# A graph network kernel: 125 instead of 100 of every 500 nodes are summed from gathered rows, and the rest from counts

## The chip, the core and the metric

The kernel runs on one core of a Trainium2 chip. The metric is the device time of one execution in microseconds; below it is the median of three runs. Stretches and single instructions are read from one execution that was profiled.

## What is computed

There are 12,500 nodes with 64 features, and 212,500 directed edges (src, dst, 16 attributes), sorted by dst. Each of three layers is a convolution; after the first two comes a ReLU, and the result of the third is added to x and normalized per row:

```
m = concatenate([h[dst], h[src], edge_attr], axis=1) @ W + b
conv(h) = segment_sum(m, dst, 12500)
h = relu(conv(x, W1, b1)); h = relu(conv(h, W2, b2)); out = layernorm(x + conv(h, W3, b3))
```

Since W acts on sums as well as on single rows, the kernel needs three things per node: the sum of the source rows over its incoming edges, the sum of their attributes, and its degree times its own row.

## The kernel before, in words

The nodes are cut into 100 tiles of 125 (`TILES`, `L`) and 25 batches of four tiles, 500 nodes (`BATCHES`, `B`). A step g is a batch in a layer, 75 steps in all. The sum over sources is made in two ways.

For the first 400 nodes of a batch (`DENSE`) it is a product with a matrix of counts: `blocks[:, k, t, s]` says how many edges go from each of the 125 nodes of tile t to node s. The source rows are held as three bf16 parts (`parts`), and per tile TensorE does one wide matmul with the first two parts (`apply_wide`, L1093) and one narrow one with the third (`apply_narrow`, L1101), narrow ones alternating between the two halves of the array. All add up in one PSUM bank. The counts are built once, during layer 0, for the next batch while the present one is applied: VectorE makes a key mask for a chunk of 5 nodes (`make_key`, L909; every fifth time `make_low`, L899), TensorE multiplies the two masks (`build_chunk`, L1074), ScalarE writes 101 pieces of 5 fp8 values (`keep_counts`, L779). That is 80 builds a batch. When a batch is complete, ScalarE's queue stores it to DRAM (`store_counts`, L787), and in layers 1 and 2 SP's queue loads it back in four quarters (`load_block`, L554), two batches ahead.

For the last 100 nodes (`FAR` = 2 groups of `GW` = 50) the source rows are gathered: GpSimd issues `J` = 8 indirect DMAs per group, one edge per partition each (`gather_rows`, L673), and TensorE multiplies them with a mask of the targets (`sum_far`, L1125 wide and L1129 narrow). In layers 1 and 2 `gather_batch` puts three pauses of two plain operations each among the 16 gathers (`rest`, L682).

The attributes are summed in layer 0 in ten groups of 50 nodes. SP loads a group three ahead (`load_group`, L578 and L584, a ring of four), GpSimd splits it into three bf16 parts (`split_attr`, L700, L702, L705, L707), VectorE makes the mask (`make_mask`, L926), TensorE sums eight times (`sum_attr`, L1114).

Order is written out by hand. In layer 0 TensorE goes through ten units of ten tiles with eight builds among them; a unit ends with the narrow matmuls and one attribute group, the last one with `sum_far` too. The first four builds of the next batch are done ahead of its first apply. VectorE goes through 80 keys and does other work at given keys: `keep_acc` of the batch before at key 1 (L948, it waits for `far_summed`, and TensorE's next apply waits for it), `keep_attr` at 6, `keep_h` at 11, `look` at 18, `make_nodes` at 53 (L974), masks at 5, 13, 21 and so on. GpSimd splits group k, issues two gathers, and ends with `make_rows` of the batch before (L717, rows times degrees for the next layer) and `scale_rows` (L728). In layers 1 and 2 each step of GpSimd is `gather_batch(g + 1)` and then, up to the first step of layer 2, `make_rows(g - 1)`; the gathers wait until the far sums two batches before are done. ScalarE copies the accumulator and the own rows (L804, L806), and then waits for `make_rows` with the store of the rows; the next batch's copy is queued behind it. TensorE's `conv` (L1154, L1155) of a batch comes in the second and third quarter of the next one and waits for those copies.

A group that has more edges than its 1,024 slots is found by `flags`, and a slow branch then does the whole work.

## Time and profile before

| | us |
|---|---|
| median of 3 runs | 3171.07 (3166.14 to 3173.89) |
| the profiled execution | 3200.72 |
| its span, first to last instruction | 3198.8 |
| TensorE busy (matmul) | 2854.0, 89% |
| GpSimd busy | 2312.6, 72% |
| VectorE busy | 1467.0, 46% |
| ScalarE busy | 1245.1, 39% |

Busy time of an engine leaves out register, semaphore and DMA-issuing work. A mean duration of a matmul is longer than its distance to the next, since matmuls are pipelined. Layer 0 with the builds ends at about 1586 us, its last batch at 1634; layer 1 ends at 2426 and layer 2 at 3188.

### The profile page before, as it was taken

Reading aid. Unit: us, or ns where it says so; the run is one execution under the profiler, and the core shown is the slowest. Engines: PE = TensorE matmul, PEld = TensorE weight load, DVE = VectorE, ACT = ScalarE, POOL = GpSimd, SP = SyncE. Lnnn points to the kernel's source line nnn. Section 1 sums busy time; section 2 is a strip of 40 time slices with the busy share of each in tenths; the row PEclk is TensorE's granted clock in tenths of the full one; section 3 lists DMA queues with packets and bytes.
Section 4 is the critical chain, followed back from the end, with each engine's and each line's share of the span. In section 5 each row is a group of like instructions: output and inputs, shape, how many; then the busy total and the mean of one; then the engine's idle time right before and its main releaser. Section 6 shows DMA issues by size and latency. Waiting matters only on the chain.

```text
span 3198.8 us, 62003 instructions
## 1 busy us (share of the span) xinstructions
PE 2854.0 (89%) x22952; PEld 1707.3 (53%) x22952; DVE 1467.0 (46%) x3427; ACT 1245.1 (39%) x2139; POOL 2312.6 (72%) x2868
## 2 busy tenths in 40 slices
PE   0049999999999999999985999999999899999998
PEld 0025555555555555555553566666665556666665
DVE  5478888888888888888710110110110111111111
ACT  1058888888888888888600000000000000000000
POOL 2726888888888888878847887777774876766672
PEclk9999999999999999999997999999999999999999
DMA  2134344443535344353586899999997889999992
GB/s 53 33 76 146 105 150 114 127 138 102 162 100 161 103 141 124 108 153 100 161 209 143 203 216 213 215 217 214 216 219 194 186 204 213 210 210 215 214 212 65
DMA packets 276171, 507.31 MB, mean 159 GB/s; under 512 B 179175, under 2 KB 227650, under 8 KB 247750
## 3 DMA queue, kind: packets, MB, share of 16 engines
q1 hardware_dynamic: 174271, 289.44, 35.7%
q10 hardware_dynamic: 58404, 150.91, 16.9%
q0 software_dynamic: 43200, 62.97, 11.0%
q8 instruction: 190, 3.11, 0.5%
q14 instruction: 106, 0.87, 0.1%
HBM read 351.58 MB, written 151.51 MB: 157 GB/s over the span
## 4 chain that ended last, share of the span: by engine, by line
PE 65%; POOL 15%; DVE 6%; DMA 6%; issue 5%; ACT 2%; another core or an unknown queue 1%; SPq 0%; ACTq 0%; POOLq 0%; DVEq 0%
PE ps L1093 32%; PE ps L1101 17%; PE ps L1074 8%; POOL far_rows L673 6%; DMA dst_stage<-in_dst 5%; PE ps L1154 2%; POOL blocks L659 2%; PE ps L1155 2%; DVE is_key L909 2%; ACT blocks L779 1%; POOL attr_stage L702 1%; DVE blocks L847 1%; POOL attr_parts L707 1%; PE ps L1125 1%
## 5 line engine op out<-in xcount | busy, mean ns | idle before, releaser
L1093 PE MATMUL ps<-blocks,parts 125*128 125x400 fp8e4 x7500 | 1674.8, 337 | 7.1 <-DVE acc_sb L948 2.7
L673 POOL DMA_INDIRECT far_rows<-parts,far_src x1200 | 1257.5, 1048 | 460.3 <-issue 322.5
L779 ACT ACTIVATE blocks<-ps 125x505 fp8e4<-125x505 f32 x2000 | 1161.8, 733 | 216.5 <-PE ps L1074 182.3
L1093 PEld LDWEIGHTS ps<-blocks,parts 125*128 125x128 bf16 x7500 | 748.2, 101 | 463.3 <-issue 35.4
L1074 PE MATMUL ps<-is_key,is_low 128*125 128x505 bf16 x2000 | 772.3, 392 | 78.5 <-DVE is_key L909 61.6
L1101 PE MATMUL ps<-blocks,parts 125*64 125x400 fp8e4 x7500 | 722.6, 336 | 0.1
L909 DVE TENSOR_SCALAR is_key<-from_one,parts 128x500 bf16<-128x500 f16 x2000 | 685.7, 391 | 30.6 <-PE ps L1074 26.0
L974 DVE COPY z<-ps 125x256 f32<-125x256 f32 x75 | 31.8, 424 | 1350.4 <-remote 792.9
L1101 PEld LDWEIGHTS ps<-blocks,parts 125*64 125x64 bf16 x7500 | 387.4, 110 | 320.8 <-issue 162.1
L1074 PEld LDWEIGHTS ps<-is_key,is_low 128*125 128x125 bf16 x2000 | 276.6, 139 | 333.7 <-DVE is_key L909 142.6
L804 ACT COPY acc_sb<-ps 128x500 f32<-128x500 f32 x50 | 28.8, 576 | 835.2 <-PE ps L1129 512.3
L899 DVE TENSOR_TENSOR is_low<-from_one,parts 128x625 bf16<-128x625 f16 x400 | 327.9, 820 | 36.8 <-PE ps L1074 24.3
L682 POOL TENSOR_SCALAR attr_stage<-attr_stage 128x256 f32<-128x256 f32 x300 | 260.6, 869 | 15.4
L700 POOL CAST attr_parts<-attr_stage 128x128 bf16<-128x128 f32 x250 | 96.2, 385 | 166.9 <-PE ps L1114 107.8
L707 POOL TENSOR_TENSOR attr_parts<-attr_stage,attr_parts 128x128 bf16<-128x128 f32 x250 | 175.4, 702 | 20.0
L812 ACT ACTIVATE std<-var,eps 125x4 f32<-125x4 f32 x25 | 7.4, 297 | 428.1 <-DVE var L991 412.8
L717 POOL TENSOR_SCALAR node_rows<-z,node_deg 125x64 f32<-125x64 f32 x200 | 127.8, 666 | 58.7 <-DVE z L974 51.5
L1061 PE MATMUL ps<-ident,blocks 125*128 125x125 f32 x40 | 7.2, 366 | 178.1 <-DVE blocks L890 178.1
L702 POOL TENSOR_TENSOR attr_stage<-attr_stage,attr_parts 128x128 f32<-128x128 f32 x250 | 145.3, 581 | 20.5
L806 ACT COPY own_sb<-ps 64x500 f32<-64x500 f32 x50 | 28.4, 569 | 283.0 <-PE ps L1140 264.5
L1154 PE MATMUL ps<-w_src,acc_sb 128*125 128x64 f32 x600 | 125.0, 290 | 6.7 <-ACT own_sb L806 6.7
L926 DVE SCALAR_TENSOR_TENSOR masks<-dst_stage,from_one 128x400 bf16<-128x400 int32 x200 | 114.9, 575 | 28.4 <-DMA dst_stage<-in_dst 26.7
(101 smaller groups left out, 1432.4 us busy)
## 6 DMA issues: line engine op xcount, KB each, us to landing
blocks<-counts SPq DMA_DIRECT2D x100, 1137.5 KB
counts<-blocks ACTq DMA_DIRECT2D x25, 4375.0 KB
blocks<-counts SPq DMA_DIRECT2D x100, 1050.0 KB
far_rows<-parts,far_src POOLq DMA_INDIRECT x1200
attr_stage<-in_edge_attr SPq DMA_DIRECT2D x250, 64.0 KB
blocks<-counts SPq DMA_DIRECT2D x100, 132.0 KB
counts<-blocks ACTq DMA_DIRECT2D x25, 507.8 KB
blocks<-counts SPq DMA_DIRECT2D x100, 121.9 KB
```

The lines of the kernel that those rows point to most:

```text
L673: nc.gpsimd.indirect_dma_start(far_rows[:, g % 2, h, j, :], None, parts_d[layer], bass.IndirectOffsetOnAxis(ap=far_src[:, g % BATCHES, h, ...
L682: nc.gpsimd.tensor_scalar(attr_stage[:, 2:4, :], attr_stage[:, 0:2, :], 1.0, None, ALU.mult).then_inc(rested, 1)
L702: nc.gpsimd.tensor_tensor(values, values, attr_parts[:, turn, :, 0:ED], ALU.subtract).then_inc(attr_left, 1)
L707: nc.gpsimd.tensor_tensor(attr_parts[:, turn, :, 2 * ED:3 * ED], values, attr_parts[:, turn, :, ED:2 * ED], ALU.subtract).then_inc(attr_sp ...
L717: last = nc.gpsimd.tensor_scalar(node_rows[:, g % 2, t, :], z[:, t, :], 0.0, deg[:, n:n + 1], ALU.max, ALU.mult)
L779: nc.scalar.activation(blocks[0:L, b % 2, :, n * W:(n + 1) * W], build[0:L, c % BUILD, 0:COLS].rearrange("p (t w) -> p t w", w=W), ACT.Cop ...
L899: nc.vector.tensor_tensor(is_low[:, m % 2, :, :], from_one[:, 0:L].rearrange("p (a l) -> p a l", a=1).to_broadcast([P, LOWS, L]), lows[:, ...
L909: nc.vector.tensor_scalar(is_key[:, c % KEY_RING, 0:KEYS], from_one[:, :], keys[:, b, n:n + 1], None, ALU.is_equal).then_inc(keyed, 1)
L1074: nc.tensor.matmul(build[0:L, c % BUILD, 0:COLS], is_low[:, c // LOWS % 2, c % LOWS, :], is_key[:, c % KEY_RING, 0:COLS], start=True, stop ...
L1093: nc.tensor.matmul(acc_ps(g), parts[0:L, layer % 2, t, 0:2, :].rearrange("p k d -> p (k d)"), blocks[0:L, g % 2, t, :], start=(t == 0), st ...
L1101: last = nc.tensor.matmul(acc_ps(g)[side:side + D, :], parts[0:L, layer % 2, t, 2, :], blocks[0:L, g % 2, t, :], start=False, stop=(t >= T ...
L1154: nc.tensor.matmul(z_ps[:, t, :], acc_flat[:, at], w_src[layer][:, :], start=True, stop=False)
```

## The change

A far group is now one whole tile: 125 nodes of each batch are gathered, in `FJ` = 18 gathers, and 375 are counted (`FAR`, `DENSE`). The builds are 75 a batch. The attributes are summed in six groups a batch: five near ones of 75 nodes (`NEAR`, `J` = 11) and the far one of 125 (18). The far mask is one operation, in fp8. The rows of `blocks` are 375 bytes long without padding. The pauses come at gathers 0, 6 and 12. `keep_acc` moves from key 1 to key 4. SP stores the attributes and loads rows and the far sources earlier in the batch. `make_rows` and `scale_rows` stay on GpSimd, `make_rows` behind the fifth group, `scale_rows` behind the sixth.

```diff
-    GW = 50
-    FAR = 2
-    DENSE = B - FAR * GW
+    FAR = 125
+    DENSE = B - FAR
+    NEAR = 5
+    GW = DENSE // NEAR
     BUILDS = DENSE // W
-    BLOCK = (TILES + 1) * DENSE
+    COLUMNS = (TILES + 1) * DENSE
+    BLOCK = -(-COLUMNS // 4) * 4
-    PAUSES = [0, 5, 10]
+    PAUSES = [0, 6, 12]
-    J = 8
+    J = 11
+    FJ = 18
-    PER_BATCH = B // GW
+    PER_BATCH = NEAR + 1
+    UNITS = TILES // UNIT
+    SUM_AFTER = [1, 3, 4, 6, 8, 9]
+    MASK_AT = [BUILDS * u // UNITS + 5 for u in SUM_AFTER]
+    GATHERS = [FJ * k // NEAR for k in range(NEAR + 1)]
...
-        far_rows = sb("far_rows", [P, 2, FAR, J, PARTS * D], bf16)
-        far_masks = sb("far_masks", [P, 2, FAR, J, GW], bf16)
+        far_rows = sb("far_rows", [P, 2, FJ, PARTS * D], bf16)
+        far_masks = sb("far_masks", [P, 2, FJ, FAR], fp8)
...
                     if g >= 1:
-                        if k == 1:
+                        if k == 0:
                             store_attr(sp, g - 1)
-                        elif k == 2 and g + 1 < BATCHES:
+                        elif k == 1 and g + 1 < BATCHES:
                             load_h(sp, g + 1)
-                        elif k == 3 and g + 1 < BATCHES:
                             load_far(g + 1)
...
             def gather_batch(g):
-                for i in range(FAR * J):
-                    if i in PAUSES:
+                for j in range(FJ):
+                    if j in PAUSES:
                         rest()
-                    gather_rows(g, i // J, i % J)
+                    gather_rows(g, j)
...
-                    if k < PER_BATCH - FAR:
-                        for i in range(k * FAR * J // (PER_BATCH - FAR), (k + 1) * FAR * J // (PER_BATCH - FAR)):
-                            gather_rows(g, i // J, i % J)
-                    if k == 7 and g:
+                    if k < NEAR:
+                        for j in range(GATHERS[k], GATHERS[k + 1]):
+                            gather_rows(g, j)
+                    if k == 4 and g:
                         make_rows(g - 1)
-                    if k == 8:
+                    if k == 5:
                         scale_rows(g)
...
                 nc.vector.scalar_tensor_tensor(
+                    out=far_masks[:, g % 2, :, :],
+                    in0=far_dst[:, b, :].rearrange("p (j a) -> p j a", a=1).to_broadcast([P, FJ, FAR]),
+                    scalar=float(b * B + DENSE - 1),
+                    in1=from_one[:, 0:FAR].rearrange("p (a n) -> p a n", a=1).to_broadcast([P, FJ, FAR]),
+                    op0=ALU.subtract, op1=ALU.is_equal, saturate=False).then_inc(masked, 1)
...
-                    if g >= 0 and n % BUILT == 5:
-                        make_mask(g, n // BUILT)
+                    if g >= 0 and n in MASK_AT[0:NEAR]:
+                        make_mask(g, MASK_AT.index(n))
+                    if g >= 0 and n == MASK_AT[NEAR]:
+                        make_far_masks(g)
                     if g >= 1:
-                        if n == 1:
+                        if n == 4:
                             keep_acc(g - 1)
...
+                for j in range(FJ):
+                    nc.tensor.matmul(acc_ps(g, at), far_rows[:, g % 2, j, 0:2 * D], far_masks[:, g % 2, j, :],
                                      start=(j == 0), stop=False)
+                for j in range(FJ):
                     side = j % 2 * D
...
-                        sum_attr(g, u)
-                        if u == PER_BATCH - 1:
-                            for h in range(FAR):
-                                sum_far(g, h)
+                        if u in SUM_AFTER:
+                            sum_attr(g, SUM_AFTER.index(u))
+                        if u == UNITS - 1:
+                            sum_far(g)
```

## Rows read from the trace of the kernel before

**Rows 1.** The page, part 5, ScalarE's evictions: busy us, mean ns | idle before, releaser

```profile
L779 ACT ACTIVATE blocks<-ps 125x505 fp8e4<-125x505 f32 x2000 | 1161.8, 733 | 216.5 <-PE ps L1074 182.3
```

**Rows 2.** Windows by stage: length, each engine's busy us, granted clock, DMA share, GB/s

```profile
303.50:1586.40 1282.90, 1213.01 (x9476) 726.15 (x9474) 1085.29 (x2643) 1070.33 (x1840) 1056.83 (x1474) 0.98 0.45 129
...
1862.40:2425.70 563.30, 563.30 (x4789) 341.70 (x4789) 57.15 (x133) 21.76 (x39) 413.91 (x471) 1.00 0.91 214
...
2654.90:3188.20 533.30, 533.30 (x4536) 323.52 (x4534) 73.91 (x178) 25.96 (x55) 346.81 (x372) 1.00 0.86 195
```

**Rows 3.** Groups of TensorE by shape: busy us, mean ns | idle before, releaser

```profile
L1093 PE MATMUL ps<-blocks,parts 125*128 125x400 fp8e4 x7500 | 1674.8, 337 | 7.1 <-DVE acc_sb L948 2.7 <-issue 2.2 <-ACT blocks L779 1.9
...
L1114 PE MATMUL ps<-masks,attr_parts 128*49 128x50 bf16 x1600 | 75.4, 186 | 4.4 <-POOL attr_parts L707 4.4
L1125 PE MATMUL ps<-far_masks,far_rows 128*128 128x50 bf16 x1200 | 57.4, 187 | 44.0 <-DMA far_rows<-parts,far_src 43.9
...
L1140 PE MATMUL ps<-ident,h_rows 125*64 125x125 f32 x300 | 46.3, 277 | 0.8 <-issue 0.8
```

**Rows 4.** Timeline of TensorE in layer 1: start, length, what, count

```profile
1943.32 4.56 PE L1093 MATMUL ps<-blocks,parts 125*128 125x400 fp8e4 x26
1947.82 2.39 PE L1101 MATMUL ps<-blocks,parts 125*64 125x400 fp8e4 x26
1950.14 0.38 PE L1125 MATMUL ps<-far_masks,far_rows 128*128 128x50 bf16 x8
...
1951.24 4.24 PE L1093 MATMUL ps<-blocks,parts 125*128 125x400 fp8e4 x24
```

**Rows 5.** Timeline of TensorE at a batch boundary of layer 0

```profile
911.50 0.64 PE L1074 MATMUL ps<-is_key,is_low 128*125 128x505 bf16 x2
914.67 1.11 PE L1074 MATMUL ps<-is_key,is_low 128*125 128x505 bf16 x2 [2.54 <-DVE is_key L909]
915.57 1.87 PE L1093 MATMUL ps<-blocks,parts 125*128 125x400 fp8e4 x5
```

**Rows 6.** Timeline of VectorE before and at that boundary

```profile
900.56 0.56 DVE L926 SCALAR_TENSOR_TENSOR far_masks<-far_dst,from_one 128x400 bf16<-128x400 int32 x1
...
907.05 0.83 DVE L899 TENSOR_TENSOR is_low<-from_one,parts 128x625 bf16<-128x625 f16 x1
907.80 0.86 DVE L909 TENSOR_SCALAR is_key<-from_one,parts 128x500 bf16<-128x500 f16 x2
913.68 0.68 DVE L948 COPY acc_sb<-ps 128x500 f32<-128x500 f32 x1 [5.03 <-remote]
```

**Rows 7.** Timeline of ScalarE's queue at that boundary

```profile
910.90 0.77 ACTq L787 DMA_DIRECT2D counts<-blocks  x2
```

**Rows 8.** Timeline of GpSimd, layer 1: first gather, and one steady batch

```profile
1671.89 1.04 POOL L673 DMA_INDIRECT far_rows<-parts,far_src  x1 [24.26 <-issue]
...
2010.81 1.03 POOL L673 DMA_INDIRECT far_rows<-parts,far_src  x1 [1.49 <-PE ps L1129]
2012.14 0.94 POOL L673 DMA_INDIRECT far_rows<-parts,far_src  x1 [0.30 <-issue]
...
2034.63 2.43 POOL L717 TENSOR_SCALAR node_rows<-z,node_deg 125x64 f32<-125x64 f32 x4 [0.35 <-issue]
...
2040.46 1.02 POOL L673 DMA_INDIRECT far_rows<-parts,far_src  x1 [1.50 <-PE ps L1129]
```

**Rows 9.** Groups of GpSimd in the window 310 to 1580 us

```profile
L673 POOL DMA_INDIRECT far_rows<-parts,far_src x364 | 451.7, 1241 | 90.9 <-issue 77.2 <-PE ps L1114 1.5
L707 POOL TENSOR_TENSOR attr_parts<-attr_stage,attr_parts 128x128 bf16<-128x128 f32 x227 | 163.5, 720 | 18.2
...
L700 POOL CAST attr_parts<-attr_stage 128x128 bf16<-128x128 f32 x228 | 89.0, 391 | 80.9 <-PE ps L1114 56.5 <-DMA dst_stage<-in_dst 24.1
```

**Rows 10.** Timeline of GpSimd in layer 0, two-input operations of a split

```profile
865.42 0.42 POOL L702 TENSOR_TENSOR attr_stage<-attr_stage,attr_parts 128x128 f32<-128x128 f32 x1
...
866.28 2.94 POOL L707 TENSOR_TENSOR attr_parts<-attr_stage,attr_parts 128x128 bf16<-128x128 f32 x1
```

More of the change, by code:

```diff
@@ L57, in gnn_kernel @@
     BANK = 512
-    assert TABLE_Q <= BANK and COLS <= BANK and E % P and GROUPS % PER_BATCH == 0
+    assert TABLE_Q <= BANK and COLS <= BANK and E % P and NEAR * GROUP_CHUNKS * W == DENSE
     PARTS = 3
@@ L1110, in sum_attr @@
                     pe.wait_ge(attr_kept, b)
-                h = k - (PER_BATCH - FAR)
-                mask = masks[:, group % 2, :, :] if h < 0 else far_masks[:, b % 2, h, :, :]
-                for j in range(J):
-                    last = nc.tensor.matmul(attr_ps[:, k * GW:(k + 1) * GW],
-                                            attr_parts[:, group % 2, j, 0:AROWS], mask[:, j, :],
-                                            start=(j == 0), stop=(j == J - 1))
-                last.then_inc(attr_summed, 1)
@@ L1119, in sum_far @@
-            def sum_far(g, h):
-                at = slice(DENSE + h * GW, DENSE + (h + 1) * GW)
-                pe.wait_ge(masked, far_group(g, h) + 1)
-                pe.wait_ge(far_landed[g % 2], (g // 2 + 1) * FAR * J * DMA)
-                for j in range(J):
-                    nc.tensor.matmul(acc_ps(g, at), far_rows[:, g % 2, h, j, 0:2 * D], far_masks[:, g % 2, h, j, :],
+                js = J if k < NEAR else FJ
+                at = slice(k * GW, (k + 1) * GW) if k < NEAR else slice(DENSE, B)
@@ new lines, in sum_attr, with sum_far @@
+                mask = masks[:, group % 2, :, :] if k < NEAR else far_masks[:, b % 2, :, :]
+                for j in range(js):
+                    last = nc.tensor.matmul(attr_ps[:, at], attr_parts[:, group % 2, j, 0:AROWS], mask[:, j, :],
+                                            start=(j == 0), stop=(j == js - 1))
+                last.then_inc(attr_summed, 1)
+            def sum_far(g):
+                at = slice(DENSE, B)
+                pe.wait_ge(masked, far_group(g) + 1)
+                pe.wait_ge(far_landed[g % 2], (g // 2 + 1) * FJ * DMA)
+                for j in range(FJ):
+                    nc.tensor.matmul(acc_ps(g, at), far_rows[:, g % 2, j, 0:2 * D], far_masks[:, g % 2, j, :],
@@ L1126, in sum_far @@
                                      start=(j == 0), stop=False)
-                for j in range(J):
+                for j in range(FJ):
                     side = j % 2 * D
-                    last = nc.tensor.matmul(acc_ps(g, at)[side:side + D, :], far_rows[:, g % 2, h, j, 2 * D:3 * D],
-                                            far_masks[:, g % 2, h, j, :], start=False, stop=(j >= J - 2))
+                    last = nc.tensor.matmul(acc_ps(g, at)[side:side + D, :], far_rows[:, g % 2, j, 2 * D:3 * D],
+                                            far_masks[:, g % 2, j, :], start=False, stop=(j >= FJ - 2))
@@ L1160, in _ @@
             for g in range(-1, BATCHES):
-                for u in range(PER_BATCH):
+                for u in range(UNITS):
                     unit = range(u * UNIT, (u + 1) * UNIT)
@@ L1166, in _ @@
                         if g + 1 < BATCHES:
-                            for n in range(u * BUILT + i * BUILT // UNIT, u * BUILT + (i + 1) * BUILT // UNIT):
+                            t = u * UNIT + i
+                            for n in range(t * BUILDS // TILES, (t + 1) * BUILDS // TILES):
                                 if not (ahead and n < 4):
@@ L1208, in _ @@
                         elif q == 1:
-                            for h in range(FAR):
-                                sum_far(g - 1, h)
+                            sum_far(g - 1)
                         elif q == 2:
@@ L1221, in _ @@
                 if g % BATCHES:
-                    for h in range(FAR):
-                        sum_far(g, h)
+                    sum_far(g)
                 if g == BATCHES:
```

126 lines of the change are left out of this document (59 added, 67 removed).

## The prediction

> **What bounds the kernel now.** I read the page first, then the kernel in windows by stage [rows 2], because a share of the whole span hides that three engines take turns. In layer 0 (303.5 to 1586.4 us, 23 batches by the copies of L948) a batch takes 1282.9/23 = 55.8 us; TensorE is busy 95% of it, VectorE 85%, ScalarE 83%, GpSimd 82%, so none is far from being the bound. In the steady part of layer 1 (563.3 us, 19 batches) and of layer 2 (533.3 us, 18 batches) a batch takes 29.65 us, TensorE is never idle at granted clock 1.00, and GpSimd looks free (73% and 65%). That last number misleads: each gather is followed by 0.30 us in which the engine counts as idle ("issue") [rows 8]. The reader is to see in [rows 8] that in layer 1 GpSimd starts a batch of gathers at 2010.81 and the next at 2040.46, and that only 1.50 us of these 29.65 are a wait for TensorE. GpSimd's own work is 28.15 us a batch: it is 5% from being the bound of layer 1. Transfers take 0.91 and 0.86 of the DMA engines' time there [rows 2], without a wait that TensorE shows.
>
> At the batch boundary of layer 0 TensorE starts two chunk builds at 911.50, then idles 2.54 us until 914.67, and applies the next batch's first tile at 915.57 [rows 5]. VectorE had made two keys and was waiting in `keep_acc` until 913.68, although the last far matmul was started before 911.50 [rows 6]. ScalarE issued the store of the counts at 910.90 [rows 7]; I can't tell whether that is what holds the signal back. After such a gap 5 wide matmuls take 1.87 us, 0.33 us each against 0.17, so the clock is at its lower level, 1.2 GHz. In the layer-0 window the mean clock is 0.98, that is 4% of 1283 us at half speed, 26 us lost, 1.1 us a batch.
>
> **TensorE, per batch.** The pitch of a matmul is (length of a run minus the mean of one)/(count minus 1). Wide, 400 columns: (4.56-0.337)/25 = 0.169 us; that is 400 columns at 0.417 ns (2.4 GHz, granted clock 1.00) and 3 ns beside them [rows 3, 4]. I price every long matmul so; a chunk build of 505 columns is 0.214 us. Narrow matmuls run in pairs on two halves of the array, 13 pairs in the 2.32 us up to the next run: a pair in 0.17 us and some 0.1 us for the change of shape [rows 4].
> - Apply: 25 columns fewer in 100 wide and 50 narrow pairs: 150 x 0.0104 = -1.56 us.
> - Far sums before: 1951.24 - 1950.14 = 1.10 us for two runs each of 8 wide and 8 narrow [rows 4]. After: 18 wide of 125 columns, 0.055 us each, with the change of shape 1.08 us; 9 narrow pairs of 0.059 us and the change 0.63 us. +0.61 us. The 0.055 is what the columns take; the ceiling is the nearest row with 125 columns, L1140, fp32: 75 runs of four in 46.3 us are 0.62 each, (0.62-0.277)/3 = 0.114 us. I take the floor, since at 50 columns the weight load of the same shape hides in 0.027 us [rows 3]; the ceiling adds 18 x 0.059 + 9 x 0.055 = 1.6 us.
> - Net in layers 1 and 2: -0.95 us, 29.65 to 28.7.
> - Layer 0 only: five builds fewer, -5 x 0.214 = -1.07. Attributes: 80 matmuls of 50 columns at 0.027 (0.38 us for eight, L1114 has a mean of 0.186) = 2.16 us become 55 of 75 columns at 0.034 and 18 of 125 at 0.055 = 2.86, +0.70; the changes of shape stay as many as the units. Net -0.95 - 1.07 + 0.70 = -1.3 us; clean work of TensorE falls from some 50.9 to 49.6 us, the other 4.9 of the 55.8 being stalls and half clock.
> - The rows of `blocks` now start every 375 bytes instead of 400, at odd addresses. No row shows such a read. Price between nothing and unknown; ScalarE already writes 5-byte pieces at odd offsets and takes 1161.8/2000 = 0.58 us [rows 1]. I take nothing and make it a rival.
>
> The Trainium skill, "TensorE: Matmul & The Clock Gate", section "Back-to-back issue gap", says that pairs of weight load and matmul sustain about 81 ns at 128 columns, not the 55 that columns alone give. It speaks against this change, which trades cheap columns in long matmuls for short ones; the 0.027 us at 50 columns [rows 3] doesn't show such a floor.
>
> **The boundary of layer 0.** `keep_acc` moves from key 1 to key 4, so the four builds that TensorE does ahead (0.86 us) no longer wait behind the copy. Before, two builds at the low clock (0.90 us) stood between the copy and the first apply; they go. The last attribute group and the far sums are 0.7 + 0.6 = 1.3 us longer, but they fill time in which TensorE idles now if the signal is held until about the same moment after the store's issue. From 4.6 us above clean work in this batch (2.54 idle, 0.5 more than normal in two late builds, and some 1.6 of half clock, of which five wide matmuls alone are 0.8) I keep 1 to 2. Over all boundaries I count -2.1 us a batch, half clock included; bounds -0.5 (only the key wait goes) and -4.
>
> **VectorE.** Near masks: 5 of 825 elements instead of 8 of 400; far mask: one of 2250 instead of two of 400. A 400-element mask takes 0.56 us [rows 6]. If 0.15 us of it are fixed (between nothing and all, an element costs at most 1.4 ns) 1.0 and 2.5 us: 7.5 against 5.6 us. Five keys of 0.34 and a set of lows of 0.8 us [rows 6] go, -2.5 us. Sum -0.6 us, about 46 of the new batch. The far mask stands before key 73; queued behind it are the last keys, for which TensorE waits; the ring of six keys covers some 3.4 us, the mask takes 2.5. I allow 0.2 us. It has then 5 us for waits, of which `keep_acc` takes some 4: it is as tight as before, and this, not the columns, keeps me from forecasting more.
>
> **GpSimd in layer 0.** Two more gathers: 1.24 busy [rows 9] and 0.25 idle (90.9/364) each, +3.0 us. Splits: 10 groups of 128 elements to 5 of 176 and one of 288. The four operations of a group take about 2.1 us (L700 0.391 and L707 0.720 are two of them) and 0.2 between them, 23 us a batch. If time goes with elements they become 20.4, if it is fixed 13.8; I take 18 (about a third fixed). Net -2: from 55.8 - 56.5/23 - 24.1/23 = 52.3 us of own time [rows 9] to about 50.5. This is under what I forecast for TensorE, by 1 us only. The Trainium skill, "GPSIMD Engine Reference", section "Elementwise — side-by-side cycle accounting", has 2.6 cycles an element for two inputs; as an estimate of that page 0.28 of the 0.42 us that a two-input operation of 128 elements takes without contention [rows 10] are elements, and the sum comes out at the same 18. ScalarE loses 5 x 0.58 = 2.9 us and stays below all.
>
> The attribute loads are issued three groups ahead; a group now lasts 8.7 instead of 5.5 us, so the cover grows. SP's queue issues four groups fewer a batch (eight DMAs), and one source list instead of two.
>
> Layer 0: 49.6 clean + about 2.8 of stalls = 52.4, -3.4 us a batch, x24 = -82 us. First batch of builds, paced by ScalarE: -3. Batch 24, paced by GpSimd: -3. Storing and reloading smaller counts ahead of layer 1: -2. The three are rough: five evictions of 0.58 [rows 1], two batches in which fewer splits meet more gathers, 6% fewer bytes. Together -90 (bounds -40 and -140).
>
> **Layer 1.** GpSimd's 28.15 us gain two gathers of 0.94 + 0.30: 30.65; with `make_rows` at some 2.2 instead of 2.43 us, as I take for a GpSimd that never waits, 30.4. TensorE wants 28.7. So GpSimd becomes the bound: its `make_rows` of one batch is queued behind the gathers two batches on, ScalarE's store waits for it and its copy of the accumulator is queued behind that store, and TensorE's `conv` waits for the copy. The layer begins with GpSimd behind, its first gather at 1671.89 after an idle 24.26 us [rows 8], so no lead has to be used up. 25 gather batches of 28.1 and 22 `make_rows` of 2.2 set the end, where today GpSimd waits. Today the layer ends 2425.7 - 1671.9 = 753.8 us after it; I get 700 + 49 + 3 for the copy + 16 for the half batch behind it = 768: +14 us (bounds +5, +28).
>
> **Layer 2** has no `make_rows`: GpSimd 28.1, TensorE 28.7. The two batches at its start wait for gathers, +5; 23 batches give -0.95 each, -22. -17 us (bounds 0 and -24). DMA: blocks -6%, gathers +12%, a little less in sum than the 0.91 of today.
>
> **Sum.** -90 + 14 - 17 = -93 us against the profiled execution of 3200.7 (span 3198.8). It lies 30 us above the median 3171.07; I put the same difference on the median: 3078 us.
>
> **Rivals.**
> - GpSimd binds layer 0 too. For: its margin is 1 us, and contention lengthens its operations (2.94 us instead of 0.42 in [rows 10]). Against: they may be mostly fixed. Period 54, -43 - 8 + 14 - 17: 3117 us. 0.20.
> - Short matmuls cost more than their columns. By the ceiling's half, 0.8 us in 48 batches of layers 0 and 2 and 0.5 in the attributes, +50: 3128 us. By 81 ns (the Trainium skill, as above) it would be 0.7 and 0.5, much the same. Against: 0.027 us at 50. 0.09.
> - The boundary stall and the half clock go wholly, and VectorE keeps up: period 50.2, -134: 3030 us. 0.11.
> - Slower: odd row addresses slow the streaming of `blocks`. 11,250 wide matmuls and pairs; layer 1 hides 1.5 us a batch, so above about 12 ns each beyond today's rate per column the gain is gone; at 20 ns, +225 - 38 hidden - 93 = +94: 3265 us. Against: nothing in the rows; for: nothing either. 0.07.
> - Nothing moves, because gather time given to layers 1 and 2 eats layer 0: 0.03. That the fallback branch is taken is excluded: counted from the inputs, the largest near group has 1370 edges (1408 fit), the largest far one 2222 (2304 fit).
>
> My forecast has 0.50. A difference of 0.3% (10 us) is about what the measurement can tell. Faster 0.89, same 0.04, slower 0.07. The range 3025 to 3140 leaves out the slower case and the ends of the others.
>
> **What would show it.** Right: layer 1's steady batch at 30 to 30.8 us with TensorE idle at `conv`, released by ScalarE's copy; layer 2's at 28.7; layer 0's at 52 to 52.8; L1093's mean down 10 ns; far matmuls 55 ns apart. Wrong: wide matmuls above 0.16 us apart; layer 0's `sum_attr` waiting for GpSimd's splits; a gap at the boundary still above 2 us.

## The result, and the profile after

The changed kernel takes 3157.84 us (median of 15, 3150.93 to 3166.92), the kernel before, run beside it 15 times, 3171.07. The ratio is 0.996, 95% interval 0.9946 to 0.9973: 13 us faster, where 93 were forecast. The profiled execution of after took 3159.32, its span is 3157.5.

Windows by stage of after, cut at copies of the accumulator as [rows 2] are. The columns are the stretch, its length, the busy time of TensorE's matmuls, of its weight loads, of VectorE, ScalarE and GpSimd, then granted clock, DMA share and GB/s:

```profile
301.60:1509.40 1207.80, 1161.51 (x9292) 721.01 (x9292) 1116.70 (x2409) 1023.73 (x1725) 1066.34 (x1148) 1.00 0.46 130
1800.80:2340.30 539.50, 508.25 (x4352) 325.36 (x4352) 73.32 (x102) 17.69 (x35) 442.15 (x477) 0.97 0.81 194
2616.70:3117.90 501.20, 494.87 (x4353) 319.93 (x4352) 95.91 (x153) 24.52 (x52) 404.53 (x408) 1.00 0.86 199
```

The first is 23 batches of layer 0: 52.5 us each, from 55.8 [rows 2], with the clock up from 0.98 to 1.00. The second is 17 batches of layer 1: 31.7 us each, from 29.65, and TensorE, never idle before, now is for 31 us, with a mean clock of 0.97. The third is 17 of layer 2: 29.5, from 29.65. So layer 0 came out as forecast (52.4), layer 1 not at all (30.4), and layer 2 little better than before (28.7).

TensorE at the end of a batch of layer 2, to be read against [rows 4], and GpSimd's and VectorE's groups of layer 0 (310 to 1500 us) against [rows 9] and [rows 6]:

```profile
2763.20 4.05 PE L1098 MATMUL ps<-blocks,parts 125*128 125x375 fp8e4 x24
...
2788.31 2.27 PE L1106 MATMUL ps<-blocks,parts 125*64 125x375 fp8e4 x26
2790.52 1.20 PE L1130 MATMUL ps<-far_masks,far_rows 128*128 128x125 fp8e4 x18
2791.65 0.69 PE L1134 MATMUL ps<-far_masks,far_rows 128*64 128x125 fp8e4 x18
2792.27 0.98 PE L1098 MATMUL ps<-blocks,parts 125*128 125x375 fp8e4 x5
```

```profile
L677 POOL DMA_INDIRECT far_rows<-parts,far_src x408 | 510.9, 1252 | 107.4 <-issue 96.9 <-PE ps L1120 2.1
L708 POOL TENSOR_TENSOR attr_stage<-attr_stage,attr_parts 128x176 f32<-128x176 f32 x113 | 121.9, 1078 | 9.2
...
L925 DVE SCALAR_TENSOR_TENSOR masks<-dst_stage,from_one 128x825 bf16<-128x825 int32 x114 | 114.8, 1007 | 0.0
L940 DVE SCALAR_TENSOR_TENSOR far_masks<-far_dst,from_one 128x2250 fp8e4<-128x2250 int32 x22 | 54.8, 2493 | 0.0
```

From 2763.20 to 2792.27 is TensorE's own batch, 29.07 us. Masks cost 1.01 and 2.49 us where 1.0 and 2.5 were forecast, a gather in layer 0 1.25 where 1.24 was. L708 is one of four operations of a split; the eight rows of splits add up to 380.5 us, 16.8 a batch, forecast 18.

Layer 1's long waits in after (engine, what it waited for, us, times, longest), 1800.8 to 2340.3 us:

```profile
ACT acc_sb L808 <- POOL node_rows L721: 490.0, 16, 31.0
...
PE ps L1159 <- ACT own_sb L810: 30.0, 16, 2.5
```

That is the chain of the prediction: TensorE's `conv` waits for ScalarE, whose copy stands behind the store that waits for GpSimd's `make_rows`. GpSimd itself never waits for TensorE here. Its timeline over one batch of layer 1, to be read against [rows 8]:

```profile
1904.58 1.81 POOL L686 TENSOR_SCALAR attr_stage<-attr_stage 128x256 f32<-128x256 f32 x2
1906.66 1.09 POOL L677 DMA_INDIRECT far_rows<-parts,far_src  x1 [0.27 <-POOL attr_stage L686]
1908.05 2.51 POOL L677 DMA_INDIRECT far_rows<-parts,far_src  x1 [0.31 <-issue]
1910.86 0.94 POOL L677 DMA_INDIRECT far_rows<-parts,far_src  x1 [0.30 <-issue]
...
1924.94 1.94 POOL L721 TENSOR_SCALAR node_rows<-z,node_deg 125x64 f32<-125x64 f32 x4
```

and VectorE's in the same microseconds:

```profile
1906.90 0.43 DVE L985 TENSOR_TENSOR parts<-left,parts 125x256 bf16<-125x256 f32 x1
1907.24 2.50 DVE L940 SCALAR_TENSOR_TENSOR far_masks<-far_dst,from_one 128x2250 fp8e4<-128x2250 int32 x1
```

Seventeen gathers of this batch take 0.94 to 1.09 us, one takes 2.51. It starts 0.8 us into VectorE's 2.50 us far mask and ends at 1910.56, 0.82 us after the mask. There is one such gather in every batch of that window (17, of 2.1 to 3.2 us). In layers 1 and 2 together 46 gathers start while the far mask runs, and 45 of them end 0.81 to 0.82 us after it, whatever their start. In the steady batches of layer 1 of before (1862.4 to 2396 us), whose masks take 0.56, none takes over 1.1 us.

### The profile page after: what moved, and what is told of

The parts are those of the page before. It is cut to its first block, busy times and chain, and to the rows that moved or that the text cites. A ratio compares the mean times of both kernels' runs of the same rounds, so it can differ in the third digit from the quotient of the medians.

```text
span 3157.5 us, 59682 instructions
## 1 busy us (share of the span) xinstructions
PE 2788.2 (88%) x22952; PEld 1754.3 (56%) x22952; DVE 1570.1 (50%) x3129; ACT 1192.8 (38%) x2014; POOL 2481.3 (79%) x2618
## 4 chain that ended last, share of the span: by engine, by line
POOL 63%; issue 14%; PE 12%; DVE 8%; ACT 2%; DMA 1%; POOLq 0%; ACTq 0%; SPq 0%; DVEq 0%
POOL far_rows L677 39%; POOL attr_stage L686 8%; POOL node_rows L721 4%; PE ps L1098 4%; POOL attr_stage L708 4%; DVE is_key L917 3%; PE ps L1079 3%; PE ps L1106 2%; POOL attr_parts L710 2%; POOL blocks L663 2%; POOL attr_parts L712 2%; ACT blocks L783 1%; DVE blocks L851 1%; DVE is_low L907 1%; POOL attr_parts L706 1%
## 5 line engine op out<-in xcount | busy, mean ns | idle before, releaser
L677 POOL DMA_INDIRECT far_rows<-parts,far_src x1350 | 1489.1, 1103 | 408.7 <-issue 356.3
L1098 PE MATMUL ps<-blocks,parts 125*128 125x375 fp8e4 x7500 | 1563.6, 327 | 3.8 <-ACT blocks L783 2.1
L783 ACT ACTIVATE blocks<-ps 125x505 fp8e4<-125x505 f32 x1875 | 1111.8, 774 | 187.4 <-PE ps L1079 186.9
L1079 PE MATMUL ps<-is_key,is_low 128*125 128x505 bf16 x1875 | 716.0, 391 | 33.2 <-DVE is_key L917 31.3
L1106 PE MATMUL ps<-blocks,parts 125*64 125x375 fp8e4 x7500 | 685.8, 326 | 0.0
L1079 PEld LDWEIGHTS ps<-is_key,is_low 128*125 128x125 bf16 x1875 | 257.5, 138 | 240.0 <-DVE is_key L917 77.4
L940 DVE SCALAR_TENSOR_TENSOR far_masks<-far_dst,from_one 128x2250 fp8e4<-128x2250 int32 x75 | 187.4, 2499 | 0.0
L721 POOL TENSOR_SCALAR node_rows<-z,node_deg 125x64 f32<-125x64 f32 x200 | 156.4, 812 | 38.8 <-DVE z L977 36.7
L1159 PE MATMUL ps<-w_src,acc_sb 128*125 128x64 f32 x600 | 126.0, 292 | 52.2 <-ACT own_sb L810 52.2
L708 POOL TENSOR_TENSOR attr_stage<-attr_stage,attr_parts 128x176 f32<-128x176 f32 x150 | 154.4, 1030 | 12.4
L1159 PEld LDWEIGHTS ps<-w_src,acc_sb 128*125 128x125 f32 x600 | 90.3, 190 | 100.3 <-ACT own_sb L810 60.2
L1130 PE MATMUL ps<-far_masks,far_rows 128*128 128x125 fp8e4 x1350 | 94.0, 225 | 56.3 <-DMA far_rows<-parts,far_src 55.9
L925 DVE SCALAR_TENSOR_TENSOR masks<-dst_stage,from_one 128x825 bf16<-128x825 int32 x125 | 125.9, 1008 | 9.1 <-DMA dst_stage<-in_dst 9.1
```

Of the source, the lines that this page charges most:

```text
L677: nc.gpsimd.indirect_dma_start(far_rows[:, g % 2, j, :], None, parts_d[layer], bass.IndirectOffsetOnAxis(ap=far_src[:, g % BATCHES, j:j + ...
L708: nc.gpsimd.tensor_tensor(values, values, into[0], ALU.subtract).then_inc(attr_left, 1)
L721: last = nc.gpsimd.tensor_scalar(node_rows[:, g % 2, t, :], z[:, t, :], 0.0, deg[:, n:n + 1], ALU.max, ALU.mult)
L783: nc.scalar.activation(blocks[0:L, b % 2, :, n * W:(n + 1) * W], build[0:L, c % BUILD, 0:COLS].rearrange("p (t w) -> p t w", w=W), ACT.Cop ...
L940: nc.vector.scalar_tensor_tensor(out=far_masks[:, g % 2, :, :], in0=far_dst[:, b, :].rearrange("p (j a) -> p j a", a=1).to_broadcast([P, F ...
L1079: nc.tensor.matmul(build[0:L, c % BUILD, 0:COLS], is_low[:, c // LOWS % 2, c % LOWS, :], is_key[:, c % KEY_RING, 0:COLS], start=True, stop ...
```

## The experiments

Each was run beside the kernel before; times are medians. Over five sets of runs the kernel before took 3168.8 (e1 to e4), 3169.6 (e5 to e8), 3200.6 (e9 to e12), 3167.6 (e13 to e16) and 3199.3 us (e17, e18). Two of the sets are thus 30 us slower from the start, and compare only within themselves; what differs in their traces is told with e12.

**e1: no far mask on VectorE from the third batch of layer 1.**

```
if g >= BATCHES + 2:
    nc.vector.engine_nop().then_inc(masked, 1)
    return
```

> The changed kernel, but from the third batch of layer 1 on VectorE no longer builds the far mask (an empty instruction signals in its place, and the mask of two batches earlier is used, so the far sums of these batches are not the reference's). Theory A: the 2.50 us VectorE instruction holds back the GpSimd gather that is issued beside it (2.51 us instead of 0.94). Then all 18 gathers of a batch take 0.94, GpSimd's batch in layer 1 falls from 31.6 to about 30.1 us and in layer 2 from 29.3 to 28.1, where TensorE's own 29.1 binds: 23 x 1.5 + 24 x 0.2 = 39 us less, about 3119. Rival B: the long gather is a matter of its place in the queue (a full ring, the eighth of its batch) and not of VectorE: it stays at 2.5 us and the time at 3158. Rival C: TensorE's columns set layers 1 and 2: the time stays even where the gather shortens.

3114.27 us, ratio to before 0.9829 (0.9812 to 0.9845). No gather of layers 1 and 2 takes over 1.21 us; the batch in layer 1 is 30.1, in layer 2 29.07 without idle, both as theory A had them. B and C fall. From the first gather at 1589.60 to the last copy of layer 1 at 2354.5 are 764.9 us; the prediction had worked out 768 for this stretch, and after takes 802.6 (1588.16 to 2390.8).

**e2: the far mask in six pieces** in layers 1 and 2.

```
for lo in range(0, FJ, 3):   # g >= BATCHES
    last = nc.vector.scalar_tensor_tensor(out=far_masks[:, g % 2, lo:lo + 3, :], ...)
```

> The changed kernel with the far mask of layers 1 and 2 built by six VectorE instructions of 3 x 125 elements in place of one of 18 x 125 (six of about 0.45 us by the 825-element mask's 1.01 us). Theory A, first form (a gather waits for the instruction that runs, and gets its turn between two): no gather takes over 1.4 us, the batch in layer 1 is 30.3 to 30.8, total about 3158 - 23 x 1.1 - 5 = 3128. Theory A, second form (instructions back to back hold GpSimd as one does): the gather stays at 2.5 us, or each of two at 1.7, and the time at 3158. Rival B (place in the queue): 3158 too, but then e1 shows no gain either.

3116.93 us, 0.9841 (0.9825 to 0.9858). The first form of theory A: the batch is 30.3, no gather in layers 1 and 2 over 1.3 us, though VectorE works 2.84 us on the pieces without a gap.

**e3: rows times degrees of layer 1 on VectorE.**

```
if layer:            # in VectorE's make_nodes, after parts_ready
    dve.wait_ge(nodes_stored[g % 2], g // 2 * 2 * DMA)
    for t in range(T):
        last = nc.vector.tensor_scalar(node_rows[:, g % 2, t, :], z[:, t, :], 0.0, deg[:, n:n + 1], ALU.max, ALU.mult)
    last.then_inc(nodes_ready, 1)
```

> The changed kernel with the rows times degrees of layer 1 made by VectorE (four more instructions in its make_nodes) in place of GpSimd. Theory A (GpSimd's own work sets layer 1): 1.94 us less for each of 25 batches, which would be 29.7 us a batch, near TensorE's own 29.1, so 24 x 1.9 = 46 us less, about 3112; a little less if the new VectorE instructions hold back gathers as the far mask does. Rival C (TensorE's columns or the landing of rows set the batch): at most 5 us less, 3153 to 3158.

3103.77 us, 0.9808 (0.9785 to 0.9832), 8 us better than expected: the batch of layer 1 is 29.6, and the batch behind the first one of the layer takes 30.1 instead of 55.4, since GpSimd does not stop for rows between its first gather batches. The long gather is still there in layer 1 (2.1 to 2.8 us).

**e4: the kernel before once more.**

> The kernel before, unchanged, one more profiled execution. The profiled execution of before took 3200.72 us and its median is 3171.07, that of after 3159.32 with a median of 3157.84. If the 30 us are chance of that one execution, this one lies within 10 us of 3171 and the 30 us sit in one or two places of the trace (layer 0's batch of 55.8, the start, a layer's start); if profiling costs this kernel 30 us, it lies at 3200 again.

3162.82 us, span 3160.9: chance, or rather a condition, not the price of profiling. Layer 0's batches are 53.0 to 53.8 us with five of 56.4 to 59.9, against the 55.8 that the prediction was built on.

**e5: before, with the accumulator copied after the fourth key.**

```
-                        if n == 1:
+                        if n == 4:
                             keep_acc(g - 1)
```

> The kernel before with one edit: VectorE copies the accumulator after the fourth key of the next batch and no longer after the first (keep_acc at n == 4). This is the part to which the prediction gave 2.1 us a batch, 50 us in all. The second profiled execution of before shows most layer 0 batches at 53.6 us with 1.5 us of idle, where the one that the prediction read has 55.8, so there is little to remove. Theory now: the move gives what is left of the boundary in a usual execution, at most 53.6 - 53.0 and the few batches of 58, 0 to 1 us a batch, 3145 to 3169. Rival (the prediction's step): 2.1 us a batch, 3119.

3165.09 us, ratio 1.0 (0.9984 to 1.0016). The rival falls. Fifteen batches are now 52.2 to 53.9 us, with a median of 52.4, but eight are 57.6 to 60.5. The waits of the two kernels for a group's data, 304 to 1500 us, e4 first:

```profile
DVE masks L926 <- DMA dst_stage<-in_dst: 18.0, 4, 5.0
```

```profile
DVE masks L926 <- DMA dst_stage<-in_dst: 56.7, 22, 7.1
```

So in a batch that waits for no group the copy's move gives before about 1.2 us (a median of 52.4 from 53.6). What the copy gave, the loads took: a quicker batch needs its groups sooner, and they don't come sooner. In the changed kernel this wait isn't in the list at all.

**e6: the changed kernel with the copy back after the first key** (the reverse edit).

> The changed kernel with keep_acc back after the first key. Theory now: layer 0's batch stays below 53.2 us, GpSimd's work of 52.5 setting it anyhow, 3158 to 3170. Rival (the prediction's step, that the move removes 2.1 us a batch of waiting at the boundary): the batch goes to 54.5 and the time to 3208.

3173.53 us, 1.0016 (1.0001 to 1.0031), 3 us above the range of the theory, which stands better than its rival. Layer 0's batch goes from 52.5 to 53.0: here the copy's place is worth 0.5 us a batch, not 2.1. The changed kernel itself took 3157.84 in one set and 3165.63 in another (e13). In the profiles layer 0 is 9.5 us longer than in after and 13.6 longer than in e13; the rest is no more than sets differ by.

**e7: the rows of `blocks` 376 bytes apart.**

```
-    COLUMNS = (TILES + 1) * DENSE
+    ROW = DENSE + 1
+    COLUMNS = (TILES + 1) * ROW
```

> The changed kernel with the rows of the count blocks 376 bytes apart and not 375, one unused byte in each, stored and reloaded with them. Rival of odd addresses: the pitch of wide matmuls falls from 161.7 ns towards 375 columns' 156 + 3 = 159, 0.4 us a batch where TensorE binds (layer 0 and 2), up to 20 us, and ScalarE's 5-byte evictions may shorten. Theory: the address costs nothing, pitch 161 to 162, time 3158 within 3.

3166.41 us, 0.9993 (0.998 to 1.0006). The wide pitch falls from 161.7 to a mean of 160.3 ns (single ones 158 to 163), and the time does not: an odd address costs 1.4 ns a wide matmul in the mean, which the time doesn't show.

**e8: e2 and e3 together.**

> The six-piece far mask and the rows on VectorE together (e2 and e3 in one). Theory: GpSimd's batch in layer 1 is then 18 gathers and three rests, 28.2 to 28.4 us, under TensorE's 29.1; both layers run at TensorE's own 29.1 without idle. From e3: 23 batches of layer 1 lose 0.5 us and 24 of layer 2 lose 0.35, 20 us less, 3084. Rival (the gains of e2 and e3 are the same microseconds): e3's 3104 stays.

3093.32 us, 0.9771 (0.9747 to 0.9796). Layer 2 is clean, 29.07, but layer 1 alternates between 29.1 and 30.1. GpSimd and VectorE there:

```profile
1998.51 1.22 POOL L677 DMA_INDIRECT far_rows<-parts,far_src  x1 [0.27 <-POOL attr_stage L686]
2000.03 3.04 POOL L677 DMA_INDIRECT far_rows<-parts,far_src  x1 [0.30 <-issue]
```

```profile
1998.77 0.96 DVE L992 TENSOR_SCALAR node_rows<-z,node_deg 125x64 f32<-125x64 f32 x4
1999.41 2.84 DVE L941 SCALAR_TENSOR_TENSOR far_masks<-far_dst,from_one 128x375 fp8e4<-128x375 int32 x6
```

The same six pieces that let the gathers through in e2 hold one here, until 2003.07, 0.82 us after the last piece (ten times in 19 batches). So pieces back to back sometimes act as one instruction.

The traces say when. The pieces start 0.46 us apart. Nearly every gather that starts inside a piece ends 0.82 us after the end of a piece, to within 0.06: of the piece in which it started, all through e2, and of the last one for eleven gathers of e8. Those eleven all started 0.15 to 0.16 us into a piece; of the others in both runs only four started 0.15 to 0.17 us into one. So what differs between e2 and e8 is at which point of a piece the gathers start, and the rows on VectorE shift that point.

**e9: each piece waits for the one before.**

> As e8 (rows on VectorE, far mask in six pieces), but each piece of the mask waits for the end of the one before, which leaves VectorE some 0.03 to 0.1 us free between two. In e8 a gather that was started inside the row of pieces took 3.0 to 3.5 us in 10 of 19 batches of layer 1 and ended 0.8 us after the last piece, in e2 none did. Theory (GpSimd gets its turn only when VectorE pauses): no gather over 1.5 us, GpSimd's batch 28.2, both layers at TensorE's 29.1 without idle, 20 x 0.45 = 9 us less than e8, 3084. Rival (a pause so short doesn't help, or the four rows operations are what holds it): as e8, 3093.

Eight of its ten executions took 3202 to 3217 us, two 3141 and 3164; the median is 3206.93 beside 3200.57, and I take nothing from the time. In its profile no gather takes over 1.5 us, as the theory had it, but layers 1 and 2 are not at 29.07: they take 792.0 and 770.0 us, where e15, which has the same edit in a set where before takes 3168, takes 768.2 and 747.0. TensorE is busy 488 of 500 us in layer 1 (1900 to 2400), and most of its gaps have no engine to wait for.

**e10: e9's kernel with no pauses between the gathers.**

> e9 without the three pauses (two GpSimd instructions of 0.9 us each, and their waits, 2.1 us in all) in a batch of gathers. If GpSimd's own work still sets a stretch, that is the two gather batches at the start of each layer, it gains up to 6 us a batch of gathers there: 4 x 6 = 24 us less, 3060. Rival (the transfers or their descriptors set the gathers' pace): each gather gets longer or the rows land as late as before, within 5 us of e9.

3973.05 us, 1.2413 (1.2384 to 1.2441). Neither theory. The gathers keep their 0.94 us, but a batch of layer 1 takes 46 us, the granted clock there is 0.80 (1989 to 2635 us), and GpSimd then waits 23 to 25 us in each for TensorE. TensorE, in the middle of its narrow matmuls, with no engine to wait for:

```profile
2139.08 0.32 PE L1117 MATMUL ps<-blocks,parts 125*64 125x375 fp8e4 x1 [1.06 <-issue]
2139.79 0.32 PE L1117 MATMUL ps<-blocks,parts 125*64 125x375 fp8e4 x1 [0.39 <-issue]
2141.20 0.32 PE L1117 MATMUL ps<-blocks,parts 125*64 125x375 fp8e4 x1 [1.09 <-issue]
```

What TensorE lacks there no row shows.

**e11: before, with the later copy and groups loaded four ahead** (`RING` 5, `n == 4`).

> The kernel before with the accumulator's copy after the fourth key (as e5) and the groups' attributes and targets loaded four groups ahead instead of three (a fifth buffer). In e5 the batches without a stall fell to 52.3 us, but VectorE waited 57 us for groups that landed late (22 times), before 18. Theory: the store of the counts, issued at each boundary, holds the loads behind it up for some 20 us, three groups of 5.5 us don't cover that, four do; then the batch is 52.4 to 52.8 nearly everywhere, 22 x 1.9 = 42 us less: 3125. The change would have this gain without being meant for it, as its groups last 8.7 us. Rival: the loads are late whatever the lead, by the DMA engines' load: 3165.

3160.14 us beside 3200.57, 0.987 (0.9842 to 0.9898). No wait for groups is left, and the batches are even, 53.0 to 54.4 us but for one of 56.1. **e17** is the same kernel again:

> The kernel of e11 once more (before, copy after the fourth key, groups loaded four ahead). Where before takes about 3168: if late groups are what its batches of 58 to 60 wait for, all batches are 52.4 us, 23 x 2.1 = 48 us less, 3120 to 3128. If e11's 40 us were all the boundary stall of that call, 3155 to 3168. If before takes about 3200 again: 3160 as in e11.

3154.63 beside 3199.34, 0.9858 (0.9841 to 0.9876). Before took 3200 again, so it repeats e11 and doesn't separate the lead from the boundary, as it was meant to.

**e12: the changed kernel with groups loaded two ahead** (`RING` 3).

> The changed kernel with the groups loaded two groups ahead instead of three: 2 x 8.7 = 17 us of lead, as much as the kernel before has with three groups of 5.5. The mirror of e11. Theory: VectorE and GpSimd wait for late groups again, 40 to 60 us in sum over layer 0, and the time is 3180 to 3200. Rival: no wait for groups, 3158 to 3166.

3246.06 us beside 3200.57, 1.0148 (1.0123 to 1.0172). Not for the reason given: one wait for a group in all (8.1 us). (The shorter ring also makes the operations of a pause read and write other buffers.) Its batches are 56 us, and those of e9 and e10, in the same set and with the full lead, are too. Up to the end of layer 0 the program of e9 and e10 is that of the changed kernel, so they show its layer 0 in such a set: the last copy starts at 1634.6 and 1637.3 us, where it starts at 1633.6 in the profile of before that the prediction read. What differs from a usual set is the boundary. The last far matmuls and VectorE's copy in e12:

```profile
1081.20 0.69 PE L1134 MATMUL ps<-far_masks,far_rows 128*64 128x125 fp8e4 x18
```

```profile
1083.45 0.68 DVE L951 COPY acc_sb<-ps 128x500 f32<-128x500 f32 x1 [2.93 <-remote]
```

and in e13, the changed kernel in a usual set:

```profile
1032.77 0.69 PE L1134 MATMUL ps<-far_masks,far_rows 128*64 128x125 fp8e4 x18
```

```profile
1033.50 0.68 DVE L951 COPY acc_sb<-ps 128x500 f32<-128x500 f32 x1 [1.59 <-PE ps L1134]
```

The matmuls end at 1081.89 and 1033.46. The copy, which by the program waits for these matmuls and an earlier `conv`, starts 1.56 us later in the one and 0.04 in the other; what releases it in e12 the profile can't name ("remote"). Over 23 boundaries the median of this lag is 0.04 us in e4, e13, e16 and the profile of after; 2.2 us in e9, e10 and e12, 1.5 in e11 and e17, and 1.4 in the profile of before that the prediction read. So those 3200.7 us are an execution of the slower kind.

**e13: the changed kernel again**, and **e16: before again**, in one set.

> The changed kernel again, beside before on the same chip. Theory: the time of layer 0 depends on the chip. Where before takes about 3170 (as on the two chips of e1 to e8), after takes 3155 to 3162; where before takes about 3200 (as on the chip of e9 to e12, layer 0's batch 55.8 in every variant of after), after has batches of 55.8 too and takes 3157 + 22 x 3.3 = 3230, slower than before. Rival (the difference lay in e9 to e12's edits): after at 3158 on any chip.

> The kernel before, profiled on the chip of e13 to e15. Theory: batches of 53.6 in layer 0 if this chip's time for before is 3160 to 3175, of 55.5 or more if it is about 3200.

3165.63 beside 3167.59, ratio 0.9987 (0.9973 to 1.0001); before was usual here, so the first half holds and the second stays untried. This set and the one of e9 to e12 ran on the same chip, so it isn't the chip alone that decides. e16 took 3179.7, with batches of 53.0 to 59.0 and nine waits of VectorE for groups (37.4 us). e4, 17 us shorter, has four of these waits (18.0 us), so they account for the range of before within a set as far as these two profiles go.

**e14: the store of the counts eleven evictions later**, on the changed kernel; **e18**, the same on before.

```
for n in range(BUILDS):
    keep_counts(b, n)
    if n == 10 and b:
        store_counts(b - 1)
```

> The changed kernel with ScalarE issuing the store of a batch's counts eleven evictions (some 7 us) into the next batch and not right at the boundary. Theory that the store at the boundary holds back the signal for keep_acc (the copy waits 2 to 4 us there): the wait is gone, 0.5 us a batch less where the chip shows batches of 52.5, 12 us, 3146, and 3 us a batch less where it shows 55.8, 70 us. Rival (the stall is the clock or VectorE's own queue): no difference to after on the same chip.

> The kernel before with one edit: ScalarE issues the store of the counts eleven evictions into the next batch. If the store at the boundary is what delays the accumulator's copy and the groups' loads: the copy's wait falls, the loads that were issued ahead of the boundary land in time, but those issued some 8 us later meet the store instead, so between no change and 48 us less: 3120 to 3168, with the sum of VectorE's waits for groups as the measure (18 to 37 us in before). If it is not the store: 3168 and the waits as in before.

e14: 3161.88, 0.9972 (0.9954 to 0.9991), as e13 to within their intervals; there was no lag to remove in that set. e18, in the other set at 3200: 3288.19 beside 3199.34, 1.0276 (1.0256 to 1.0296), batches of 59 us. The median lag at the boundary falls to 0.9 us, but waits for groups grow to 50.3 us on VectorE and 77.2 on GpSimd. With the store moved the groups land later; whether it also causes the lag, these runs only hint at.

**e15: e9 and e14 together.**

> All together: rows of layer 1 on VectorE, far mask in six pieces each waiting for the last, the counts' store eleven evictions later. Theory: layers 1 and 2 at 29.1 us a batch without idle, as e9; layer 0 as e14: 3075 where before takes 3170, and at most 3110 where before takes 3200. Rival: the late store collides with the loads of the groups, and layer 0 gets the late landings of e5 back, 3100 or more.

3079.50 us, 0.9708 (0.9683 to 0.9734), the fastest kernel of this study, 4 us above what was expected. Windows of 20 batches of layer 1 and 22 of layer 2:

```profile
1742.60:2324.00 581.40, 581.40 (x5121) 376.20 (x5120) 119.15 (x300) 22.87 (x41) 456.61 (x474) 1.00 0.89 212
2431.40:3071.00 639.60, 639.60 (x5634) 413.93 (x5634) 141.13 (x302) 31.74 (x67) 502.57 (x521) 1.00 0.84 196
```

29.07 us a batch and not a moment of idle TensorE in either. Its gathers take at most 1.5 us.

## Why the prediction was wrong

By the copies of the accumulator, us from the last one of the stage before to the last of this one:

| stage | before, read for the prediction | before, e4 | after | forecast | measured against the first, against e4 |
|---|---|---|---|---|---|
| start and layer 0 | 1633.6 | 1605.7 | 1553.4 | -90 | -80, -52 |
| layer 1 | 792.1 | 789.4 | 837.4 | +14 | +45, +48 |
| layer 2 | 762.5 | 755.2 | 756.1 | -17 | -6, +1 |
| sum | | | | -93 | -41, -3 |

Against the execution that it read, the prediction misses by 52 us; another 28 are the step from there to the median. Three of its steps failed: the boundary's -2.1 us a batch, the far mask's effect on GpSimd, which it had at nothing, and the difference put on the median.

**The boundary, and the sum's last step.** "I put the same difference on the median": the 30 us between the profile and the median belonged to before's layer 0. The lag of 1.4 us from the last far matmul to the copy is in that profile and not in e4 or e16, nor in after. With it goes the largest single term, the boundary's -2.1 us a batch, 50 us: moved alone, the copy gives before nothing in sum (e5), and moved back it costs after 0.5 us a batch (e6). Nor does like against like give the -90: where the lag exists, the changed layer 0 of e9 and e10 ends 1 and 4 us later than before's.

Layer 0 of after is 52 us faster than e4's all the same. By the copies, 22 us are the 23 batches (52.5 us where e4's without a late group take 53.5), 24 are what e4's five batches of 56 to 60 take beyond that, 5 are the last batch and 1 the start. Against e16 it is 20, 41, 6 and 1. In a batch without a late group TensorE's own work did fall as forecast (1.3 us): it is busy 50.3 us in e13, 51.4 in e5's. But it now waits 2.1 us for VectorE's keys (L1079), 0.9 in e5, and so both take 52.4. VectorE is busy 49.6 us a batch in e13 where about 46 were forecast; a key has a mean of 438 ns there and 389 in e4 (310 to 1500 us). GpSimd was priced 2 us too low as well, though gathers and splits came out as forecast: the four operations of `make_rows` were left at their price, and L721 has a mean of 1.11 us (L717 in before: 0.75). In the profile of after, TensorE's wait is from the ninth batch on one of 1.3 us for the splits of L712 and one of 0.7 for keys, at 52.6; in e13 it waits for splits in the last batch alone.

That late groups are gone from after, 24 to 41 us, the prediction had at nothing, though it saw that the lead of the loads grows. That e5's kernel has no late group with a longer lead is shown, in two sets at 3200 (e11, e17). That the longer lead is also what spares after is not: e12 cut it to 17 us, and one wait of 8.1 us came back. After also issues fewer loads and stores smaller counts, and which of these does it is open.

**Layer 1: the far mask's effect on GpSimd was missing.** +14 was right for everything that was in it: without the mask the stretch from the first gather takes 764.9 us where 768 was worked out (e1), and GpSimd's batch 30.1 against 30.4. Missing were 1.57 us a batch. The mask was priced on VectorE alone, at 2.5 us, which it takes; that a long instruction there holds back a gather here was not asked. 25 x 1.57 is 39 us, and e1 gives 38 back in this stretch. A sign of it stood in the rows: a gather takes 1.24 us in layer 0 [rows 9], where VectorE is busy 85%, and 0.94 in layer 1 [rows 8], where it is busy 10%. The operation of 2.94 us instead of 0.42 [rows 10] may be a case of it too: VectorE works without a gap all the while, 866.28 to 869.22. The prediction called it contention and left it in layer 0. The Trainium skill, "SBUF — State Buffer", section "SBUF: two separate sides", says that VectorE and GpSimd share a pair of ports that one of them holds for a whole instruction while "the other fully blocks", and names a VectorE operation with two SBUF inputs as a case, against a GpSimd operation that reads SBUF. A box in that section says that GpSimd's DMAs wait with their descriptors for a VectorE operation in a 2-port performance mode; of one with two inputs it doesn't speak. The trace agrees with the first, and shows it for a DMA that GpSimd issues: the gather ends 0.82 us after the single mask, and by the same 0.82 in e3. Of six pieces in a row a gather waits for one in e2, and for all that are left in the eleven cases of e8.

**Layer 2** failed for the same reason: GpSimd's 28.1 became 29.3 with a gather of 2.1 us in each batch, and so the bound. TensorE's own batch is 29.07, not 28.7: the wide pitch is 161.7 ns where 159 was forecast, 0.4 us over 150 matmuls and pairs, of which e7 puts half on odd addresses. The start of the layer cost 5 us, as forecast (the first two batches against e4's).

**What held.** Layer 0's batch (52.5 against 52.4), in part by luck: it is 50.3 us of work and 2.1 of waits for keys, where 49.6 and 2.8 were added up, and the 2.1 us of gain at the boundary that led there weren't to be had. GpSimd bound in layer 1, with the waits in the order given. Far matmuls: in after 1.20 us for a run of 18, a pitch of 0.057 us against 0.055 forecast; the 81 ns of the Trainium skill ("TensorE: Matmul & The Clock Gate", "Back-to-back issue gap") don't appear, and that rival falls. The first rival, GpSimd bound in layer 0 too, was at most half right: in one of two profiles TensorE waits for the splits, at a period of 52.6, not 54. Odd addresses: no (e7). The boundary stall wholly gone, 50.2 us: no, VectorE's copy still waits 2.1 us a batch for TensorE.

**Open.** Whether the change is a loss where the lag exists. The changed kernel itself ran in no set at 3200. e12 says so (+1.5%), with the shorter lead, which no wait makes responsible. The stages say so too: layer 0 no shorter (e9, e10) and layer 1 longer by 44 us (e12: 836.2 against before's 792.1), which with layer 2's -5 is about 3240 us against 3200, my estimate. What makes a set so is open, and so is why TensorE has the gaps of e9 there.

## What to carry to other kernels

Read a stall of a microsecond in a second execution before building a sum on it: the largest term here was a property of one profile, and the check is one pair of rows, end of the producer and start of the consumer. When VectorE gets one long instruction in place of several short ones, look at what GpSimd does in those microseconds, its DMA issues included; cut the instruction into pieces, so that what GpSimd issues is held for one piece at most times. Gaps between the pieces came with no gather over 1.5 us (e9, e15), but in these two runs only two gathers started at the point of a piece that e8's held ones share, so that the gaps are what helps is not shown. And price a lead of loads as a term of its own: in e5 a faster batch used it up, and its gain turned into waits for data.

## What the runs showed of the hardware

- A gather that GpSimd starts while VectorE runs an instruction of 2.50 us with two inputs ends 0.82 us after that instruction, whenever it started (45 of 46 in after), and takes 2.1 to 3.2 us instead of 0.94. Of six such instructions back to back, 2.84 us in sum, it waits for the one in which it started (e2), but for the last one in eleven cases of e8, all started 0.15 to 0.16 us into a piece.
- With no pauses between the gathers TensorE has stretches of matmuls 0.7 us and more apart with no engine to wait for, and the kernel is 24% slower than before (e10); e9, which differs by the pauses alone, is not. The pauses of 2.1 us, three a batch, are not idle time to be saved. Why is not shown.
- The same kernel, in two of five sets of runs, has a lag of 1.4 to 2.2 us, instead of 0.04, from the end of the matmul that signals to the start of the copy that waits, at the batch boundaries of layer 0, and is 30 us slower there (before: 3200 against 3168). One chip gave both kinds of set.
